# Unread TensorE products beside delta's nine-row products, and the first state's scan ahead of the second batch's carries

## The reference

```python
xb, z = split(x @ in_w.T)                       # 256 + 256 columns
xb = silu(conv(xb) + cb)                        # causal, four taps
delta, Bm, Cm = split(xb @ xp_w.T)              # 8 + 16 + 16 columns
delta = softplus(delta @ dtw.T + dtb)
dA = exp(delta[..., None] * -exp(a_log))
mi = delta[..., None] * Bm[:, :, None, :] * xb[..., None]
v = 0.6 * v + mi_t                              # momentum, along the tokens
h = dA_t * h + v                                # state, along the tokens
y = einsum(h, Cm) + dp * xb                     # 16 states summed
out = (y * silu(z)) @ ow.T
```

## Time and profile before

| | |
|---|---|
| median of 3 runs | 1099.54 us (1098.83 to 1100.37) |
| the profiled execution: its time | 1098.12 us |
| its span, first to last instruction | 1096.8 us |
| inputs of layer 0, in the span | about 418 to 487 us |
| states of layer 0 | from about 487 us |
| inputs of layer 1 | about 661 to 738 us |
| TensorE busy | 93% of the span |
| VectorE busy | 89% |
| ScalarE busy | 75% |
| granted TensorE clock, mean | 0.959 |

### The profile page before, as it was taken

The page is one execution under the profiler, slowest core; times in us unless marked ns, Lnnn a source line. Parts: engine busy times, 40 slices in busy tenths (PEclk is TensorE's granted clock), DMA queues, the critical chain, the costliest instruction groups (busy, mean ns, idle before and its releaser), DMA issues. The chain is left out here.

```text
span 1096.8 us, 21387 instructions
## 1 busy us (share of the span) xinstructions
PE 1019.9 (93%) x7821; PEld 639.0 (58%) x7821; DVE 970.9 (89%) x1307; ACT 824.6 (75%) x1607; POOL 520.5 (47%) x488
## 2 busy tenths in 40 slices
PE   6899999999999978889999999899999996779997
PEld 3122222222222334458998895458888894579996
DVE  5989999999996688979999997879999999888885
ACT  4289999999999646988898863988888870558761
POOL 4501401010101352027898993028999994247773
PEclk9679999999999999999999999899999999779999
DMA  4230100001000533107999990106999994922223
GB/s 120 68 94 16 31 16 24 23 17 31 17 2 2 136 78 59 60 1 192 239 253 227 221 245 9 63 1 164 213 254 240 213 256 135 293 55 74 73 70 127
DMA packets 60328, 121.04 MB, mean 110 GB/s; under 512 B 15486, under 2 KB 28798, under 8 KB 59968
## 3 DMA queue, kind: packets, MB, share of 16 engines
q0 software_dynamic: 15440, 52.66, 24.1%
q1 hardware_dynamic: 43170, 64.98, 19.0%
q10 hardware_dynamic: 1614, 2.04, 0.6%
HBM read 58.02 MB, written 13.19 MB: 65 GB/s over the span
## 5 line engine op out<-in xcount | busy, mean ns | idle before, releaser
L2315 PEld LDWEIGHTS m_pair<-filter_w,delta_x_t 128*128 128x128 f32 x2560 | 294.9, 193 | 42.2 <-issue 42.2
L2315 PE MATMUL m_pair<-filter_w,delta_x_t 128*128 128x112 f32 (+3 forms) x2560 | 299.4, 276 | 8.7 <-DVE h_t L2342 3.3
L571 DVE TENSOR_REDUCE neg_max<-max_ps 128x1 f32<-128x1024 f32 x256 | 293.2, 1215 | 11.2 <-PE max_ps L560 11.0
L688 ACT ACTIVATE exp_scores<-score_k 128x512 f32<-128x512 f32 x512 | 274.0, 599 | 16.8 <-PE score_k L680 9.6
L2291 ACT ACTIVATE decay<-delta,a_log 128x1024 f32<-128x1024 f32 x128 | 145.7, 1142 | 49.3 <-DVE normed L2342 28.8
L560 PE MATMUL max_ps<-k_rows,q_rows 48*128 48x512 bf16 x512 | 167.3, 405 | 6.2 <-DVE neg_max L571 5.1
L2283 ACT ACTIVATE filter_w<-filter,b_t 128x112 f32<-128x112 f32 (+1 forms) x576 | 167.4, 374 | 0.0
L708 PE MATMUL score_k<-exp_scores,v_cols 128*32 128x256 f32 x2048 | 164.5, 395 | 0.0
L680 PE MATMUL score_k<-q_rows,k_rows 51*128 51x512 bf16 x512 | 163.3, 390 | 0.4 <-DMA q_rows<-neg_max_rows 0.4
L580 POOL CAST neg_max_parts<-neg_max 128x16 bf16<-128x16 f32 x16 | 3.1, 197 | 234.6 <-DVE neg_max L571 234.6
L560 PEld LDWEIGHTS max_ps<-k_rows,q_rows 48*128 48x128 bf16 x512 | 29.9, 95 | 120.0 <-DVE neg_max L571 91.1
(11 more groups left out here) (348 smaller groups left out, 1732.1 us busy)
## 6 DMA issues: line engine op xcount, KB each, us to landing
c_row<-c_rows SPq DMA_DIRECT2D x64, 512.0 KB, 6.0
x_inner<-normed POOLq DMA_DIRECT2D x16, 512.0 KB, 6.6
delta_x<-mod_memory POOLq DMA_DIRECT2D x15, 512.0 KB, 8.0
delta_x<-x_inner POOLq DMA_DIRECT2D x15, 512.0 KB, 8.0
x_inner<-h_t POOLq DMA_DIRECT2D x14, 512.0 KB, 5.7
mod_memory<-h_t POOLq DMA_DIRECT2D x14, 512.0 KB, 9.1
mod_memory<-normed POOLq DMA_DIRECT2D x12, 512.0 KB, 8.6
gate_up_all<-in_gate_up_w SPq DMA_DIRECT2D x8, 512.0 KB, 7.3
```

Source lines behind the costliest of these rows:

```text
L571: ve.tensor_reduce(nm[leg % 2][:, 4 * j + qt:4 * j + qt + 1], mps[:, bank:bank + 2, :].rearrange("p a q -> p (a q)"), AX_X, ALU.max, negat ...
L688: ac.activation(pt[a % 4][:, HEADS[r % 4], :], eps[:, bank, :], ACT.Exp, scale=SC).then_inc(*exped.up())
L2315: mm = pe.matmul(vps[blk][:, lo:hi], self.duT[b][:, c, blk * P:(blk + 1) * P], wf[g % 3][:, lo:hi], start=True, stop=True)
```

## The change

1. **Unread products.** A new `pe_unread(rows)` multiplies `rows` rows of the identity by as many rows of `in_w` (512 columns) into the ring's next bank, when that is free, without taking it; nobody reads it, and the next taker overwrites it. One of 64 rows (partitions 0 to 63) stands between the two nine-row products of each of the eight `pe_delta`; one of 128 rows stands ahead of the first `pe_delta` of layer 0, one ahead of `turn(2)` of layer 0, and one ahead of the `du_turn` of batch 0 in layer 1. That makes eleven.
2. **The first state's scan.** `ve_scan_first(0, 0)` is issued within `mamba_inputs`, ahead of `ve_carry(1)`, and no longer in the loop. Its output goes to `h_first[0]`, in the SBUF tile `mod_memory`, since the ring is still in use; `ve_output` reads it there. In layer 1 `pe_momentum(0, 0, 0)` moves ahead of `pe_c(1)`, as it stands in layer 0 already.
3. **The filter.** In layer 0 `ac_filter(0, 0)` moves ahead of the evacuations of four gate products. For that the first state uses the third slot of `wf`, which is moved by eight columns to lie behind `hp`.

```diff
@@ class Ring
+    def next(self):
+
+        i = self.turn % len(self.tiles)
+        return self.tiles[i], (self.free[self.first + i], self.used[self.first + i])
@@ mamba_memory
-        flat = sb("filter_w", [P, 3 * S])
+        flat = sb("filter_w", [P, 3 * S + 8])
-        self.wf = [flat[:, k * S:(k + 1) * S] for k in range(3)]
+        self.wf = [flat[:, k:k + S] for k in (0, S, 2 * S + 8)]
@@ mamba_inputs
+        def pe_unread(rows):
+
+            ps, open_ = ring.next()
+            wait_from(pe, *open_)
+            pe.matmul(ps[:], self.ident[0:rows, :], iw[0:rows, 0, :], start=True, stop=True)
+
@@ pe_delta
             for c in range(2):
+                if c:
+                    pe_unread(2 * R2)
@@ layer 0
+            pe_unread(P)
             pe_delta(0, 1)
...
+            pe_unread(P)
             turn(2)
...
+            ac.wait_ge(*bands[0][0])
+            ac_filter(0, 0)
             ac_g(0)
             ac_g(3)
...
-            ac.wait_ge(*bands[0][0])
-            ac_filter(0, 0)
...
             pe_momentum(0, 0, 0)
+            ve_scan_first(0, 0)
             pe_c(1)
@@ layer 1
             ve_softplus(1, 1)
+            pe_unread(P)
             for k in (2, 6, 8):
                 du_turn(0, k, ac_du_turn)
...
             ac_decay(0, 0)
+            pe_momentum(0, 0, 0)
+            ve_scan_first(0, 0)
             pe_c(1)
             ac_filter(0, 1)
-            for blk in range(NBLK):
-                pe_momentum(0, 0, blk)
+            pe_momentum(0, 0, 1)
@@ mamba_scan
-                w = ac.activation(wf[g % 3][:, lo:c * STEP + P], tri[min(c, 1)][:], ACT.Copy,
+                w = ac.activation(wf[(g - G0 + 2) % 3][:, lo:c * STEP + P], tri[min(c, 1)][:], ACT.Copy,
...
+            elif g == G0:
+                to = h_first[0]
+                if 0 in first_read:
+                    ve.wait_ge(*first_read[0])
...
-            ve.tensor_tensor(to, hps[:], csb[g % 3][:], ALU.mult).then_inc(*ys.up())
+            ve.tensor_tensor(to, h_first[0] if g == G0 else hps[:], csb[g % 3][:], ALU.mult).then_inc(*ys.up())
...
-            ve_scan_first(b, n)
+            if i:
+                ve_scan_first(b, n)
```

More of the change, by code:

```diff
@@ L1613, in ve_rms_norm, with mamba_inputs @@
             self.rms_normed[t] = self.normed.at()
-    def mamba_inputs(self, l, in_w, tail, ac_filter, ac_decay, pe_momentum, po_skip):
+    def mamba_inputs(self, l, in_w, tail, ac_filter, ac_decay, pe_momentum, po_skip, ve_scan_first):
         pe, ve, ac, po, sp = self.pe, self.ve, self.ac, self.po, self.sp
@@ L2315, in pe_momentum @@
                 mm = pe.matmul(vps[blk][:, lo:hi], self.duT[b][:, c, blk * P:(blk + 1) * P],
-                               wf[g % 3][:, lo:hi], start=True, stop=True)
+                               wf[(g - G0 + 2) % 3][:, lo:hi], start=True, stop=True)
             mm.then_inc(*vmm.up())
@@ L2472, in mamba_scan @@
         first_done = None
-        self.mamba_inputs(l, in_w, tail, ac_filter, ac_decay, pe_momentum, po_skip)
+        self.mamba_inputs(l, in_w, tail, ac_filter, ac_decay, pe_momentum, po_skip, ve_scan_first)
         for g in range(3):
```

## The result

The changed kernel takes 1113.77 us (median of 4 runs, 1112.45 to 1118.97), the kernel before 1099.18 us (4 runs, 1096.58 to 1100.37): a ratio of 1.0148, 95% interval 1.0121 to 1.0174. It is 14.6 us slower, where 5.3 us faster was predicted and the range ended at 1098.4 us.

The account below looks back on a forecast made before the run. VectorE's waits for TensorE, partly at half clock, were taken to bound the kernel. Terms 0.4 + 2.8 + 1.7 + 0.6 - 0.1 = 5.4 us, 5.3 us taken: 1099.5 - 5.3 = 1094.2 us, range 1091.5 to 1098.4 us.

Parts of the forecast that it names:

- Unread products, their cost: Both layers: 128-row products fit pauses free, 64-row ones run beside the pairs; 0.1 us lost, at most 1.8 us.
- My other end: Delta's pairs, both layers: the 64-row products run one after the other, 0.9 us each, at most 1.8 us at two places.
- the fillers take their own time: Rival, delta's pairs: three products cannot share the array, 1.8 us more at two places, 1095.9 us; chance 0.09.
- Clock at 437 to 440 us and 707 to 716 us: Turns in layer 0, turns and carries' products in layer 1: fillers keep full clock, gaining 0.4 us and 1.7 us.
- Scan ahead of the carries, layer 0: First state: first product with C 1.75 us earlier, TensorE then at full clock; 2.8 us gained by the second state.
- The same in layer 1: First state's scan ahead of the carries in layer 1: product with C 2.3 us earlier, 0.6 us of it newly counted.
- Filter ahead of four evacuations: Layer 0, batch 1 turns and first momentum: momentum keeps its time, 0, between 0.5 us earlier and 0.8 us later.
- Full products in pauses: Three 128-row products in TensorE's pauses, both layers: each fits and costs nothing; 0.9 us each if a pause is gone.
- The one on the slower side: Rival: clock falls within the loops, 9 us at half clock costs about 6.5 us, 1100.7 us; chance 0.05.
- The fillers do not hold the clock: Rival, both layers: 0.4 and 1.7 us go, the reorder stays, 3.3 us gained, 1096.2 us; chance 0.15.

Follow-up runs that it names:

- rows32: The change with 32 rows instead of 64 in each unread product between a pair; 1095.03 us, ratio 0.9967 to the kernel before.
- full128: The change with each of the eight unread products between a pair widened from 64 to 128 rows; ratio 1.0135 to the kernel before.
- order_alone: The change with all eleven unread products taken out, the reorder kept; 1094.66 us against 1098.32 us before, ratio 0.9968.
- before_again: The kernel before, unchanged, profiled once more; executed once for its trace, no run time given.
- filter_back: The change without unread products and with layer 0's first filter back behind the four gate evacuations; ratios 0.9987 and 0.9989 to the kernel before.
- mixed: The change without products within pairs, layer 0's two full products replaced by 64 with 32 rows and 64 with 64; executed once for its trace, no time.
- pauses_only: The change with the eight 64-row products within pairs taken out, the three of 128 rows kept; 1096.58 us, ratio 0.9993 to before.

## Why the prediction was wrong, step by step

**Unread products, their cost: this step failed.** "I take them as a third product side by side: 0.05 us where a reader waits." The row behind it was of two products of nine rows, each of which counts as one group of 32 rows (rows32 has them side by side with 32 rows); a product of 64 rows is of another size, and between the two sizes TensorE runs one after the other. What the runs showed in its place: 1.05 us of own time for each filler, and the pair parted by it, 3.2 us for 1.13 us. My other end, 0.9 us each, left out that the pair is parted, and I counted two places where a reader waits. In fact five stages grew (A, B, C, F and G), B and G beyond anything that the kernels without unread products show. The rival "the fillers take their own time" had the mechanism and was sized at 1.8 us; rows32 gives the whole difference of 64 to 32 rows: from 1.0148 to 0.9967, 19.9 us of 1099.

**Clock at 437 to 440 us and 707 to 716 us: failed, and undone by the first step.** The fillers were to hold the clock. It fell again near 438, 458 and 721 us, and in layer 1 at a new place, 694 us, while products of 9 and 64 rows ran one after the other; against full128 that stage took 7.4 us more, most of it by the fall. The carries' products of layer 1 did take 3.61 us, but the 1.7 us did not come: a fall at 721 us covered the turns ahead of them, and H was shorter by 0.23 us only. In order_alone and before_again H was 1.68 us shorter, with no filler: it is how the falls wander. The prediction read the length of four falls in one execution as belonging to the code.

**Scan ahead of the carries, layer 0: right in mechanism and mostly in size.** 1.75 us predicted for the first product with C, 1.54 us measured (filter_back). For the second state I had 2.8 us; filter_back shows D at 2.84 us, but 1.30 us of it is the fall at 488 us, which before_again did not have either. So the move is worth 1.54 us, and the other 1.30 us only against an execution in which the clock falls there.

**The same in layer 1:** 0.6 us predicted, 0.15 us measured (I, and the same in order_alone). The scan began about where the sum had it, 5.49 us behind the copies (746.70 - 741.21; the sum had 729.7 - 724.4 = 5.3 us). But the carries took 3.69 us from 748.90 us on, and the product with C waited 0.40 us more behind them; the sum had 3.6 us for both.

**Filter ahead of four evacuations:** 0 predicted, between 0.5 us earlier and 0.8 us later. Where the clock was alike (mixed against filter_back), the first product with C came 0.67 us earlier, a little beyond the early bound: the copies were late by 0.32 us, but the momentum no longer waited for the filter.

**Full products in pauses:** free, as predicted, where the pause is still there. In the change two of the three pauses were gone.

**The rivals.** The one on the slower side named a loss of the clock in the loops; E is -0.06 us. The loss was elsewhere and by another mechanism. Its sum was off as well: 9 us at half clock can cost TensorE 4.5 us at most, not 6.5 us, so such a fall would not have eaten the 5.3 us. (The terms of the forecast add up to 5.4 us, of which 5.3 us was taken.) "The fillers do not hold the clock" came true too; at its own price it would have left the kernel 3.3 us faster.

## What to carry to other kernels

Here products ran side by side on TensorE only where they used the same number of groups of 32 rows. Before one is put beside or between others, look whether its rows come to the same size (32, 64 or 128), or give it rows that do. And the length of a clock fall in one trace is not a property of the code; profile the same kernel twice before a term is built on it, and compare a stage only between executions in which the clock was the same there.

## What the hardware showed that was not expected

- A switch between products of 64 and of 9 or 32 rows on disjoint partitions costs the whole overlap: 1.05 us a product where three of 32 rows start within 0.02 us. Two of 64 rows overlap as well as two of 32 (1.13 us for four records).
- The same code had a low clock for 3 us in one execution and for 6 to 7 us in another at 437 and 457 us, and none at 488 us where the other had it. Stages moved by 1.3 to 2.2 us with that.
- The loop over the states (E) was up to 1.71 us longer in some executions with no lower clock seen in it. In pauses_only it arises in the last 12 us of the loop: VectorE waits 0.57 us for the transfer of a row of C at 649.80 us, and 1.48 us (0.19 us before) at 661.61 us for ScalarE, which itself had waited for a transfer into `mod_memory`. Why the transfers were late is open.
